# Three attention and feed-forward blocks on one core: who normalises the layer norm's rows, and how the output projection's parts are held

## The reference, cut to what matters

```python
def layer_norm(x, g, b):
    mu = jnp.mean(x, axis=-1, keepdims=True)
    var = jnp.mean(jnp.square(x - mu), axis=-1, keepdims=True)
    return (x - mu) * jax.lax.rsqrt(var + EPS) * g + b

def cross_attention(x, ctx, wq, wk, wv, wo, bo):
    q, k, v = (heads of x @ wq, ctx @ wk, ctx @ wv)
    scores = jnp.einsum('bhnd,bhmd->bhnm', q, k) * SCALE
    out = jnp.einsum('bhnm,bhmd->bhnd', jax.nn.softmax(scores, axis=-1), v)
    return jnp.einsum('bnf,fe->bne', out, wo) + bo

x = cross_attention(layer_norm(x, g1, be1), layer_norm(x, g1, be1), wq1, wk1, wv1, wo1, bo1) + x
x = cross_attention(layer_norm(x, g2, be2), context, wq2, wk2, wv2, wo2, bo2) + x
```

## Time and profile before

| what | value |
|---|---|
| median of three runs | 1448.77 us (1447.6 to 1449.91) |
| the profiled execution, its own time | 1451.27 us |
| its span, first to last instruction | 1449.5 us |
| PE busy | 1318.3 us, 91% |
| DVE busy | 1035.4 us, 71% |
| POOL busy | 812.7 us, 56% |
| ACT busy | 742.8 us, 51% |

### The profile page before, as it was taken

One profiled execution on the slowest core, in us unless ns is written; L12 is line 12 of the kernel. 1 busy time (PEld: TensorE's weight loads), 2 busy tenths in 40 slices (PEclk: granted clock), 3 DMA queues, 4 the chain that ended last, 5 costly groups with the idle time before them and its releaser, 6 DMA issues. The chain is left out here.

```text
span 1449.5 us, 38973 instructions
## 1 busy us (share of the span) xinstructions
PE 1318.3 (91%) x16460; PEld 1125.8 (78%) x16460; DVE 1035.4 (71%) x1902; ACT 742.8 (51%) x1356; POOL 812.7 (56%) x832
## 2 busy tenths in 40 slices
PE   4999899886999999999978999999999999999587
PEld 3777777764888888889966888888888888888587
DVE  4577777756778877887647787878787878776485
ACT  2356666552545544554524655555555555554354
POOL 2266777665645544545515656555555556566364
PEclk9588999966999999999977999999999999999799
DMA  5001110002000000000010000000010000000000
GB/s 133 12 11 47 47 33 2 2 2 66 2 2 2 2 2 2 2 2 2 2 40 7 2 7 2 7 2 7 2 46 2 2 2 2 2 2 2 12 15 24
DMA packets 31959, 20.36 MB, mean 14 GB/s; under 512 B 21415, under 2 KB 30315, under 8 KB 31787
## 3 DMA queue, kind: packets, MB, share of 16 engines
q1 hardware_dynamic: 31786, 17.86, 4.9%
HBM read 16.54 MB, written 1.31 MB: 12 GB/s over the span
## 5 line engine op out<-in xcount | busy, mean ns | idle before, releaser
L521 POOL TENSOR_TENSOR cross_probs_l<-cross_probs 128x1024 f16<-128x1024 f32 x160 | 303.3, 1895 | 95.0 <-ACT cross_probs L593 94.0
L593 ACT ACTIVATE cross_probs<-cross_score 128x1024 f32<-128x1024 f32 x160 | 164.1, 1025 | 230.4 <-PE cross_score L837 230.4
L690 DVE TENSOR_REDUCE cross_top<-cross_max 128x2 f32<-128x1024 f32 x160 | 194.5, 1216 | 9.4 <-PE cross_max L811 9.2
L1610 POOL TENSOR_TENSOR ad_probs_l<-ad_probs 128x1024 f16<-128x1024 f32 x64 | 121.0, 1894 | 94.5 <-ACT ad_probs L1687 93.9
L593 ACT ACTIVATE self_probs<-self_score 128x1024 f32<-128x1024 f32 x80 | 82.1, 1026 | 148.6 <-PE self_score L837 148.6
L521 POOL TENSOR_TENSOR self_probs_l<-self_probs 128x1024 f16<-128x1024 f32 x80 | 152.2, 1903 | 2.0 <-ACT self_probs L593 1.6
L857 PEld LDWEIGHTS cross_pv<-cross_v_h,cross_probs 128*128 128x128 bf16 x1280 | 117.2, 98 | 34.0 <-issue 26.3
L857 PE MATMUL cross_pv<-cross_v_h,cross_probs 128*128 128x65 bf16 x1280 | 136.4, 196 | 2.9 <-POOL cross_probs_l L521 2.8
L858 PE MATMUL cross_pv<-cross_v_l,cross_probs 128*128 128x64 f16 x1280 | 134.9, 195 | 0.0
L859 PE MATMUL cross_pv<-cross_v_h,cross_probs_l 128*128 128x65 bf16 x1280 | 134.5, 194 | 0.0
L676 DVE TENSOR_TENSOR cross_qk_l<-cross_shared,cross_qk_h 128x256 fp32r<-128x256 f32 (+1 forms) x160 | 88.0, 556 | 56.0 <-ACT cross_qk_h L578 55.6
(11 more groups left out here) (426 smaller groups left out, 4869.5 us busy)
## 6 DMA issues: line engine op xcount, KB each, us to landing
ad_ctx_rows<-in_ctx SPq DMA_DIRECT2D x8, 192.0 KB, 2.9
cross_ctx_rows<-in_ctx SPq DMA_DIRECT2D x8, 192.0 KB, 2.5
sw_raw<-in_L_xattn_wq SPq DMA_DIRECT2D x2, 640.0 KB, 6.1
sw_raw<-in_L_xattn_wk SPq DMA_DIRECT2D x2, 640.0 KB, 4.4
sw_raw<-in_L_xattn_wv SPq DMA_DIRECT2D x2, 640.0 KB, 3.9
cw_raw<-in_L_xattn_wq SPq DMA_DIRECT2D x2, 640.0 KB, 4.1
lr_raw<-in_L_xattn_w_ff SPq DMA_DIRECT2D x2, 640.0 KB
out<-x_rows SPq DMA_DIRECT2D x8, 160.0 KB, 1.9
```

The costliest lines, as they stand in the source:

```text
L521: nc.gpsimd.tensor_tensor(probs_l[:, n % PR, :, :].rearrange("p j k -> p (j k)"), whole, whole.bitcast(BF16)[:, 1::2], ALU.subtract).then_ ...
L593: nc.scalar.activation(probs[:, n % PR, :, :].rearrange("p j k -> p (j k)"), score_bank[:, :], ACT.Exp, scale=SCALE).then_inc(exped, 1)
L690: nc.vector.reduce_max(out, scores, AX.X).then_inc(max_read, 1)
L1610: nc.gpsimd.tensor_tensor(probs_l[:, n % PR, :, :].rearrange("p j k -> p (j k)"), whole, whole.bitcast(BF16)[:, 1::2], ALU.subtract).then_ ...
```

## The change

Layer norm of both attentions. `inverse_root` on GpSimd also makes `neg_mean` (minus the mean) and `offset` (minus the mean times the reciprocal root). ScalarE normalises, with four activations of scale `rstd` and bias `offset`, at the end of the first round of slot 3; VectorE no longer does. ScalarE also copies `ln_t` to `ln_h`, straight behind the two activations that make `ln_t`. VectorE makes the low parts by two operations of 128 partitions: a subtraction for `ln_l`, and h * m + `ln_t`, where the column m is -1 for the rows that take a low part and 0 for the others.

Output projection of both attentions. `attn_th` and the weights' high part are bfloat16, `attn_tl` and the weights' low part float16. Three matmuls of 160 columns for each chunk go into the same 160 columns, and VectorE adds once.

```diff
-        self.wo_hl = sb("wo_hl", [P, NCH, 2, HID], F32R)
+        self.wo_h, self.wo_l = sb("wo_h", [P, NCH, HID], BF16), sb("wo_l", [P, NCH, HID], F16)
...
-        attn_th = sb("attn_th", [P, NCH, SEQ], F32R)
-        attn_tl = sb("attn_tl", [P, NCH, SEQ], F32R)
+        attn_th = sb("attn_th", [P, NCH, SEQ], BF16)
+        attn_tl = sb("attn_tl", [P, NCH, SEQ], F16)
...
                 pool.wait_ge(var_eps_ready, b + 1)
+                nc.gpsimd.tensor_tensor(neg_mean[:, :], mean_var[:, :, 0], neg[:, :], ALU.mult)
                 nc.gpsimd.tensor_tensor(rstd[:, :], var_eps[:, :], half_neg[:, :], ALU.pow).then_inc(rstd_ready, 1)
+                pool.wait_ge(rstd_ready, b + 1)
+                nc.gpsimd.tensor_tensor(offset[:, :], neg_mean[:, :], rstd[:, :], ALU.mult).then_inc(offset_ready, 1)
...
                 nc.scalar.activation(ln_t[:, 1, :], bank_[:, SEQ:2 * SEQ], ACT.Identity, bias=shift[:, 1:2],
                                      scale=gain[:, 1:2]).then_inc(lnt_ready, 1)
+                act.wait_ge(lnt_ready, b + 1)
+                nc.scalar.copy(ln_h[b % 2][:, :, :], ln_t[:, :, :]).then_inc(ln_hi, 1)
+
+            def normalise(b):
+                act.wait_ge(offset_ready, b + 1)
+                for t in range(QT):
+                    row, scaled = x[:, b * QT + t, :], dict(bias=offset[:, t:t + 1], scale=rstd[:, t:t + 1])
+                    nc.scalar.activation(xn[:, t, 0, :], row[:, 0:HA], ACT.Identity, **scaled)
+                    ins = nc.scalar.activation(xn[:, t, 1, :].rearrange("p (r f) -> p r f", r=REP),
+                                               row[:, None, HA:HID].to_broadcast([P, REP, HB]), ACT.Identity, **scaled)
+                ins.then_inc(xn_ready, 1)
...
-                    dve.wait_ge(lnt_ready, b + 1)
-                    nc.vector.tensor_copy(h[:, :, :], ln_t[:, :, :]).then_inc(emptied, 1)
-                    dve.wait_ge(emptied, ring.read(kind, period, key))
-                    nc.vector.tensor_tensor(low[:, :], ln_t[:, 0, :], h[:, 0, :], ALU.subtract)
-                    nc.vector.tensor_tensor(h[HB:2 * HB, 1, :], ln_t[HB:2 * HB, 1, :], h[HB:2 * HB, 1, :], ALU.subtract)
-                    nc.vector.tensor_tensor(h[3 * HB:P, 1, :], ln_t[3 * HB:P, 1, :], h[3 * HB:P, 1, :],
-                                            ALU.subtract).then_inc(ln_ready, 1)
+                    dve.wait_ge(ln_hi, b + 1)
+                    nc.vector.tensor_tensor(low[:, :], ln_t[:, 0, :], h[:, 0, :], ALU.subtract).then_inc(emptied, 1)
+                    nc.vector.scalar_tensor_tensor(h[:, 1, :], h[:, 1, :], low_rows[:, 0:1], ln_t[:, 1, :],
+                                                   ALU.mult, ALU.add).then_inc(ln_ready, 1)
...
-                    nc.vector.tensor_tensor(row, bank_[:, 0:HID], row, ALU.add).then_inc(part_ready, 1)
-                    dve.wait_ge(part_ready, b * QT + i + 1)
-                    nc.vector.tensor_tensor(row, bank_[:, HID:2 * HID], row, ALU.add).then_inc(emptied, 1)
+                    nc.vector.tensor_tensor(row, bank_[:, 0:HID], row, ALU.add).then_inc(emptied, 1)
...
+                    rows, passes = slice(i * P, (i + 1) * P), ((attn_th, wo_h), (attn_th, wo_l), (attn_tl, wo_h))
                     for k in range(NCH):
-                        rows = slice(i * P, (i + 1) * P)
-                        nc.tensor.matmul(bank_[:, 0:2 * HID], attn_th[:, k, rows], wo_hl[:, k, :, :].rearrange("p a n -> p (a n)"),
-                                         start=k == 0, stop=False)
-                        mm = nc.tensor.matmul(bank_[:, 0:HID], attn_tl[:, k, rows], wo_hl[:, k, 0, :], start=False, stop=k == NCH - 1)
+                        for n, (lhs, rhs) in enumerate(passes):
+                            mm = nc.tensor.matmul(bank_[:, 0:HID], lhs[:, k, rows], rhs[:, k, :], start=k == 0 and n == 0,
+                                                  stop=k == NCH - 1 and n == 2)
```

More of the change, by code:

```diff
@@ L183, in operands @@
         if w == "o":
-            return self.raw_o, self.wo_hl[:, :, 0, :], self.wo_hl[:, :, 1, :], slice(0, P)
+            return self.raw_o, self.wo_h[:, :, :], self.wo_l[:, :, :], slice(0, P)
         raw = self.raw[part]
@@ L260, in __init__ @@
         raw = stack.enter_context(nc.sbuf_tensor("lr_raw", [P, 4 * DFF], F32, side="right"))
-        self.wo_hl = stack.enter_context(nc.sbuf_tensor("lr_wo_hl", [P, NCH, 2, HID], F32R, side="right"))
+        self.wo_h = stack.enter_context(nc.sbuf_tensor("lr_wo_h", [P, NCH, HID], BF16, side="right"))
+        self.wo_l = stack.enter_context(nc.sbuf_tensor("lr_wo_l", [P, NCH, HID], F16, side="right"))
         self.gain, self.shift = (stack.enter_context(nc.sbuf_tensor(f"lr_{what}", [P, 2], F32, side="right")) for what in ("gain", "shift"))
@@ L386, in attention @@
         wq, wk, wv = weights.q, weights.k, weights.v
-        wo_hl = background.wo_hl if cross else weights.wo_hl
+        wo_h, wo_l = (background.wo_h, background.wo_l) if cross else (weights.wo_h, weights.wo_l)
         gain, shift, bo_row = weights.gain, weights.shift, weights.bo_row
@@ L392, in attention @@
         half_neg = sb("half_neg", [P, QT], F32)
+        neg = sb("neg", [P, QT], F32)
+        neg_mean = sb("neg_mean", [P, QT], F32)
+        offset = sb("offset", [P, QT], F32)
+        low_rows = sb("low_rows", [P, 1], F32)
         eps = sb("eps", [P, QT], F32)
@@ L443, in attention @@
         rstd_ready = sem("rstd_ready")
+        offset_ready = sem("offset_ready")
         xn_ready = sem("xn_ready")
         lnt_ready = sem("lnt_ready")
+        ln_hi = sem("ln_hi")
         ln_ready = sem("ln_ready")
@@ L460, in attention @@
         x_bo_ready = sem("x_bo_ready")
-        part_ready = sem("part_ready")
         block = stack.enter_context(nc.Block())
@@ L529, in _ @@
             nc.gpsimd.memset(half_neg[:, :], -0.5)
+            nc.gpsimd.memset(neg[:, :], -1.0)
             nc.gpsimd.memset(eps[:, :], EPS).then_inc(filler, 1)
@@ L603, in slot @@
                             extra(kind, period, key, {"cur": cur, "prev": prev, "nxt": nxt}[key[1]])
+                    if s == 3 and r == 0 and nxt is not None:
+                        normalise(nxt[0])
+            normalise(0)
             for key in ring.keys["first"][:PRE]:
@@ L619, in statistics @@
                 ins.then_inc(var_ready, 1)
-            def normalise(b):
-                dve.wait_ge(rstd_ready, b + 1)
-                for t in range(QT):
-                    row = x[:, b * QT + t, :]
-                    nc.vector.tensor_scalar(xn[:, t, 0, :], row[:, 0:HA], mean_var[:, t, 0:1], rstd[:, t:t + 1],
-                                            ALU.subtract, ALU.mult)
-                    ins = nc.vector.tensor_scalar(xn[:, t, 1, :].rearrange("p (r f) -> p r f", r=REP),
-                                                  row[:, None, HA:HID].to_broadcast([P, REP, HB]),
-                                                  mean_var[:, t, 0:1], rstd[:, t:t + 1], ALU.subtract, ALU.mult)
-                ins.then_inc(xn_ready, 1)
             def extra(kind, period, key, batch):
@@ L690, in slot @@
                         nc.vector.reduce_max(out, scores, AX.X).then_inc(max_read, 1)
-                    if s == 3 and r == 0 and nxt is not None:
-                        normalise(nxt[0])
                     for at, key in items(kind, s):
@@ L711, in slot @@
                                             ALU.mult).then_inc(attn_ready, 1)
+            for n in range(REP):
+                nc.vector.memset(low_rows[n * HB:(n + 1) * HB, :], -1.0 * (n % 2))
             statistics(0)
-            normalise(0)
             for key in ring.keys["first"][:PRE]:
```

4 lines of the change are left out of this document (2 added, 2 removed).

## The result

| what | before | after |
|---|---|---|
| median, on one chip | 1449.34 us (1447.6 to 1452.71, 4 runs) | 1399.08 us (1397.93 to 1400.88, 4 runs) |
| profiled execution, its span | 1451.27, 1449.5 us | 1397.93, 1396.2 us |

The ratio is 0.964, with an interval of 0.962 to 0.967: 50 us faster, where the forecast said 40.

The account below looks back on a forecast made before the run. PE was taken as the bound, with VectorE ending its remaining waits. Terms of 16.6, 13.6, 7.1 and 3.0 us sum to 40.3 us, from the profiled 1451.3 to 1411.0, giving a median of 1408.5 us; range 1398 to 1425.

Parts of the forecast that it names:

- Output projection: Both attentions, PE: thirty 16-bit passes at 70 ns take 2.10 us instead of 2.62 per half batch; 16.6 us saved.
- ACT's additions at nothing: Four normalise activations of 0.45 us each on ACT delay nothing that PE needs; charged 0.
- Layer norm in self: Self's steady periods: attention output comes earlier, PE's 2.10 us waits shrink to 0.3, bank wait goes; 13.6 us saved.
- Layer norm in cross: Cross: VectorE's maxima start 0.8 us earlier in seven batches and the bank wait goes; 7.1 us saved.
- Start of self: Start of self attention: half of 6.0 us of waits for the layer norm's parts goes; 3.0 us saved.
- The join: End of self to slot 5 of cross: 1.0 us saved, as the forecast's terms are spread over the stretches.
- Tail: Tail and feed-forward: 1.0 us saved, as the forecast's terms are spread over the stretches.
- more comes back than the idle time shows: Rival: wider gaps than idle time, passes possibly at 63 ns, slots starting earlier; 1399 us, chance 0.10.
- The collision: Rival: VectorE's low parts in the attentions' layer norm wait for POOL's subtraction to end; 1425 us, chance 0.12.
- ACT late: Rival: activations take 0.57 us and the next exponentials gate PE, 1.0 us in each of 14 batches; 1422 us, chance 0.09.
- slow passes: Rival: output projection's 16-bit passes do not hide their weight loads; 1461 us at 125 ns a pass, chance 0.04.
- moved waits: Rival: PE is held by the next thing, exponentials or POOL's subtraction, so about nothing is won; 1448 us, chance 0.03.

Follow-up runs that it names:

- the doubled passes: The changed kernel with each output projection's thirty passes made twice into the same bank: median 1460.95 us.
- the parts alone: The kernel before with only the high part copied on ACT and the low parts made in two operations; VectorE still normalises: 1431.02 us, ratio 0.988.
- 2048 columns: The changed kernel with one VectorE write of 2048 columns ahead of slot 4's attention output in self: median 1417.30 us.

## Why the prediction was right, and where not

**Output projection: the price right, the total too high.** 16.6 us were forecast with a pass at 70 ns; it takes 69 ns, and nearly all of it is on the path (the doubled passes). Between the kernel with the layer norm alone and the changed one the six steady periods of self are 5.8 us shorter, the last one 1.0, cross 7.5: 14.3 us for 28 half batches, where 28 x 0.52 are 14.6. The join gives 1.8 us back. In all the projection brings 13.4 us on top of the layer norm and 12.0 alone.

**ACT's additions at nothing: right, by little.** 0.49 us an activation, not 0.45, but started 0.39 us apart; the exponentials of slot 4 wait for them and their reader doesn't. The next 1.5 us would have cost 12.

**Layer norm in self: 13.6 forecast, 17.5 measured** (steady periods, layer norm in self alone). The steps that failed are sizes. I kept 0.3 us of each wait of 2.1: nothing of it stayed, 6 x 0.25 us. I took the bank wait at its idle time, 0.46 us: the slot became 0.67 us shorter (4.33 to 3.66), 6 x 0.2. And a fallen clock of 1.5 us in period one was not in the sum at all, though PE's clock could be read slot by slot. (Slots 6 and 7, 0.03 us longer each, take 0.3 us back.) The split between the halves was wrong too: the collision of the cast was a consequence of `normalise`, so I had put on the parts what the two halves share.

**Layer norm in cross: 7.1 forecast, 8.9 measured.** The maxima's wait of 0.90 us gave 1.06 a period, not 0.8; the bank wait, listed with 0.2 to 0.3 us, gave 0.52.

**Start of self: 3.0 forecast, 2.7 measured**, not shown to be the layer norm's: in two kernels with self's old layer norm the first part of this stretch (48.1 us before, 45.4 after) took 49.9 us (projection alone) and 51.2 us (layer norm in cross alone), at a mean granted clock of 0.75 and 0.74 where the kernel before had 0.79.

**The join: 1.0 forecast, for the projection, 6.5 measured.** This is the largest error, and a term that the sum lacks. The time lies only 1 us under the range, so the 5.5 us missing here put it outside, but the 3.9 us missing in self would have sufficed as well. I had counted the waits of steady periods and one start, and had put nothing for the start of cross, where the same cast and the same four `tensor_scalar` stand in VectorE's queue, with PE stopping and running at 1.2 GHz around them.

**Tail: 1.0 forecast, 2.3 measured.** The projection alone gave 2.0 and the layer norm alone 2.3 us there; what they share is not separated.

**The rivals.** The one that came true, more comes back than the idle time shows, stood at 0.10 with 1399 us, close to the result. The passes at 63 ns that it counted on were no part of it; the clock was. The collision is real (1.0 us a period with the parts alone, 1.3 forecast), but the changed kernel escapes it by about 0.05 us, for the reason that I gave against it: GpSimd's subtraction comes earlier. ACT late, slow passes, and moved waits did not come.

## What to carry to other kernels

A wait that is taken away is worth its idle time plus what PE then runs slowly behind it, so beside each wait read PE's granted clock and the distance between fixed points (a slot's start to the next) and not only the list of waits; a join of two stages wants its own term. Halves of a change that stand in one engine's queue share their gain, the sum of two parts can come out right by errors that cancel, and one may only be safe with the other: run each alone before one is called useless or harmful. When runs of one kernel spread by more than the effect, compare stretches that repeat, and look whether the same code repeats in another kernel, too.

## What the runs showed of the hardware

- Behind a stop of 2.1 us PE's granted clock was at 0.50, 1.2 GHz, for some 3 us of work, at a price of 1.4 to 1.6 us (ten of twelve such waits in the kernels with the projection alone and with 2048 columns); behind stops of 1.06 us never (six). With the float32r projection it was one of six at 2.1 us in each of four executions, so length alone does not decide.
- The adapter, the same instructions in every kernel, took 324.8 to 338.8 us; the rest of the same program repeats within 0.3 us. In another program the same code need not: the join of the changed kernel took 55.9 us and, behind longer periods of self, 54.5 us with the same idle time.
- A VectorE subtraction with two SBUF inputs, or a cast with one, that would otherwise end sooner ends 0.28 to 0.29 us after the GpSimd subtraction that it started in (541.88 after 541.60, 497.78 after 497.50; the cast 505.79 after 505.50). One that started 0.1 us before GpSimd's end kept its 0.43 us.
